# Selective scan of a Mamba layer on one Trainium2 core: one scan and one product per group of three units

## What is computed

```python
dA = jnp.exp(delta[..., None] * A)
dBu = delta[..., None] * Bm[:, :, None, :] * xc[..., None]

def step(h, inp):
    dA_t, dBu_t, C_t = inp
    h = dA_t * h + dBu_t
    y = jnp.einsum('bdn,bn->bd', h, C_t)
    return (h, y)
```

## Time and profile before

| | us |
|---|---|
| three runs | 6336.2, 6339.48, 6344.21 |
| median | 6339.48 |
| profiled execution: span from first to last instruction | 6343.7 |
| busy in this span: PE, DVE, POOL, ACT | 6036.5, 5685.5, 5209.8, 5097.3 |

### The profile page before, as it was taken

The page is one execution under the profiler, slowest core; times in us unless marked ns, Lnnn a source line. Parts: engine busy times, 40 slices in busy tenths (PEclk is TensorE's granted clock), DMA queues, the critical chain, the costliest instruction groups (busy, mean ns, idle before and its releaser), DMA issues. The chain is left out here.

```text
span 6343.7 us, 99100 instructions
## 1 busy us (share of the span) xinstructions
PE 6036.5 (95%) x32260; PEld 3123.0 (49%) x32260; DVE 5685.5 (90%) x4459; ACT 5097.3 (80%) x8658; POOL 5209.8 (82%) x5092
## 2 busy tenths in 40 slices
PE   8999999999999999999999999999999999998776
PEld 5645445454554545545455544545455454554222
DVE  0089999999999999999999999999999999999998
ACT  4588888888888888888888788888888888887664
POOL 0078888888888888888888888888888888888988
PEclk9999999999999999999999999999999999998665
DMA  3367676676767667675676767667676766767553
GB/s 95 88 165 170 160 167 157 163 162 169 169 154 168 155 165 170 155 182 142 167 162 162 173 156 169 155 164 163 167 169 156 166 154 165 168 142 160 129 124 75
DMA packets 805826, 983.25 MB, mean 155 GB/s; under 512 B 391258, under 2 KB 417542, under 8 KB 805318
## 3 DMA queue, kind: packets, MB, share of 16 engines
q1 hardware_dynamic: 805318, 976.92, 65.4%
HBM read 717.71 MB, written 259.00 MB: 154 GB/s over the span
## 5 line engine op out<-in xcount | busy, mean ns | idle before, releaser
L1181 POOL TENSOR_TENSOR hc<-hs,cs 128x512 f32<-128x512 f32 x3072 | 3835.6, 1271 | 692.7 <-DVE hs L1140 505.6
L1140 DVE TENSOR_TENSOR_SCAN hs<-av,state,b 128x512 f32<-128x512 f32 x2688 | 3257.8, 1263 | 88.6 <-POOL state L1185 4.9
L1008 ACT ACTIVATE av<-rep_d,nega 128x512 f32<-128x512 f32 x3072 | 2096.7, 713 | 41.5 <-DVE hs L1140 36.8
L1134 DVE TENSOR_TENSOR b<-rep_u,pb 128x1536 f32<-128x1536 f32 x1024 | 1803.5, 1761 | 211.0 <-PE pb L846 124.7
L855 PE MATMUL py<-hc,rsel 128*32 128x512 f32 x6144 | 1141.6, 634 | 40.6 <-POOL hc L1181 39.7
L769 PE MATMUL cb<-xu,w1a 96*128 96x392 f32 x2400 | 984.3, 513 | 27.7 <-DVE b1a L1120 17.4
L774 PEld LDWEIGHTS cb<-w2c,g 128*98 128x98 f32 x9600 | 885.9, 167 | 169.7 <-issue 106.9
L774 PE MATMUL cb<-w2c,g 128*98 128x96 f32 x9600 | 910.7, 252 | 17.4 <-ACT g L956 9.3
L956 ACT ACTIVATE g<-cb,b1a 128x392 f32<-128x392 f32 x1200 | 679.5, 579 | 87.0 <-PE cb L769 78.8
L810 PE MATMUL cb<-xn,wtap 96*96 96x512 f32 x1536 | 723.3, 607 | 2.4 <-ACT xn L1029 2.4
L769 PEld LDWEIGHTS cb<-xu,w1a 96*128 96x128 f32 x2400 | 414.5, 191 | 415.4 <-issue 199.3
(11 more groups left out here) (109 smaller groups left out, 6703.4 us busy)
## 6 DMA issues: line engine op xcount, KB each, us to landing
rep_d<-delta_scratch SPq DMA_DIRECT2D x512, 384.0 KB, 7.0
rep_u<-deltax_scratch SPq DMA_DIRECT2D x512, 384.0 KB, 6.3
cs<-c_scratch SPq DMA_DIRECT2D x512, 256.0 KB, 5.9
delta_scratch<-dlt SPq DMA_DIRECT2D x128, 384.0 KB, 3.1
deltax_scratch<-dlt SPq DMA_DIRECT2D x128, 384.0 KB, 9.2
t1r<-t_scratch SPq DMA_DIRECT2D x160, 240.0 KB, 6.5
v_scratch<-v2s SPq DMA_DIRECT2D x192, 192.0 KB
xb<-in_x SPq DMA_DIRECT2D x128, 192.0 KB, 4.6
```

The source lines that it names most:

```text
L1008: act.activation(av[:, n % NAV, :], rep_d[:, k % 2, j, :], ACT.Exp, scale=nega[:, q, j:j + 1])\
L1134: dve.tensor_tensor(b3[:, :, :], rep_u[:, k % 2, 3 * hf:3 * hf + 3, :], pb[:, None, :].broadcast_to([128, 3, T]), ALU.mult).then_inc(dve_b ...
L1140: dve.tensor_tensor_scan(hs[:, n % NHS, :], av[:, n % NAV, :], b3[:, n % 3, :], start, ALU.mult, ALU.add)\
L1181: pool.tensor_tensor(hc[:, n % NHC, :], hs[:, n % NHS, :], cs[:, k % 2, g % NQ, :], ALU.mult)\
```

## The change

Three scans of 512 columns become one scan of 3 x 512 = 1536 columns over the group. To keep the units apart, column 0 of every `av` tile is set to zero once and the exponentials write columns 1 to 511; so at the first column of each unit the running value is dropped. What the unit should have carried over is put into column 0 of b instead: b[0] plus a[0] times the state. For that POOL makes `first_x` = A times the first column of the next chunk's `rep_d`, ACT its exponential `first_a`, and POOL twice a chunk `carry` = `first_a` times `state`. In chunks 1 to 7 DVE then writes column 0 of b by a new instruction (`scalar_tensor_tensor`, `rep_u` times `pb` plus `carry`, 3 columns) and the other 511 columns by the product as before. In chunk 0 the product writes all columns.

POOL multiplies the group by C in one product of 1536 columns, after the one scan. `av` grows to 9 tiles, so that a group lies in one piece; two constant tables are stored more tightly to make room. The counts of the semaphores go from units to groups.

```diff
-NHC, NAV, NHS = 6, 8, 6
+NHC, NAV, NHS = 6, 9, 6
...
-    "act": dict(xn=10, y=(18, 6), d=11, mid=23, batch=16),
+    "act": dict(xn=10, y=(18, 6), d=11, mid=23, batch=16, first=15),
     "dve": dict(),
-    "pool": dict(u=23, bc=(18, 22), y=(17, 8)),
+    "pool": dict(u=23, bc=(18, 22), y=(17, 8), first=5, carry=(14, 23)),
...
-        up_w = sb("up_w", [128, 2, GW])
+        up_w = sb("up_w", [128, GW])
...
-        wdt = sb("wdt", [128, DI])
+        wdt = sb("wdt", [128, C])
...
-        state = sb("state", [128, NG, 3])
-        zero_state = sb("zero_state", [128, 1])
+        state = sb("state", [128, NQ, NJ])
+        first_x = sb("first_x", [128, NQ, NJ])
+        first_a = sb("first_a", [128, NQ, NJ])
+        carry = sb("carry", [128, NQ, NJ])
...
             def reduce(s, k, g):
-                pe.wait_ge(pool_hc, count(pool_hc, G * NU + 3 * g + 3))
+                pe.wait_ge(pool_hc, count(pool_hc, G * NG + g + 1))
...
-                act.wait_ge(dve_h, count(dve_h, G * NU + n + 1 - NAV))
-                act.activation(av[:, n % NAV, :], rep_d[:, k % 2, j, :], ACT.Exp, scale=nega[:, q, j:j + 1])\
+                act.wait_ge(dve_h, count(dve_h, G * NG + n // 3 + 1 - NAV // 3))
+                i = (G * NU + n) % NAV
+                act.activation(av[:, i, 1:T], rep_d[:, k % 2, j, 1:T], ACT.Exp, scale=nega[:, q, j:j + 1])\
                     .then_inc(act_a, 1)
...
+                if n == AT["act"]["first"] and 0 <= st.s and k + 1 < NC8:
+
+                    c = st.s * (NC8 - 1) + k
+                    act.wait_ge(pool_first, count(pool_first, c + 1))
+                    act.wait_ge(pool_carry, count(pool_carry, c * 2))
+                    act.activation(first_a[:, :, :], first_x[:, :, :], ACT.Exp).then_inc(act_first, 1)
...
-            dve.memset(zero_state[:, :], 0.0)
+            dve.memset(av[:, :, 0], 0.0).then_inc(av_set, 1)
...
             def unit(s, k, n):
                 G = s * NC8 + k
                 hf, g, q = n // 12, n // 3, n // 3 % NQ
+                if n % 3 != 0:
+                    return
+                js = slice(3 * hf, 3 * hf + 3)
...
-                if n % 3 == 0:
-
-                    dve.wait_ge(pe_b, count(pe_b, G * NG + g + 1))
-                    dve.wait_ge(dve_h, count(dve_h, G * NU + n))
-                    dve.tensor_tensor(b3[:, :, :], rep_u[:, k % 2, 3 * hf:3 * hf + 3, :],
-                                      pb[:, None, :].broadcast_to([128, 3, T]), ALU.mult).then_inc(dve_bu, 1)
-                    dve.wait_ge(pool_st, count(pool_st, G * NG + g + 1 - NHS // 3))
-                    dve.wait_ge(dve_bu, count(dve_bu, G * NG + g + 1))
-                dve.wait_ge(act_a, count(act_a, G * NU + n + 1))
-                start = state[:, g, n % 3:n % 3 + 1] if k > 0 else zero_state[:, 0:1]
-                dve.tensor_tensor_scan(hs[:, n % NHS, :], av[:, n % NAV, :], b3[:, n % 3, :], start, ALU.mult, ALU.add)\
+                dve.wait_ge(pe_b, count(pe_b, G * NG + g + 1))
+                dve.wait_ge(dve_h, count(dve_h, G * NG + g))
+                lo = 0
+                if k > 0:
+                    lo = 1
+                    dve.wait_ge(pool_carry, count(pool_carry, (s * (NC8 - 1) + k - 1) * 2 + hf + 1))
+                    dve.scalar_tensor_tensor(b3[:, :, 0], rep_u[:, k % 2, js, 0], pb[:, 0:1], carry[:, q, js],
+                                             ALU.mult, ALU.add).then_inc(dve_c, 1)
+                dve.tensor_tensor(b3[:, :, lo:T], rep_u[:, k % 2, js, lo:T],
+                                  pb[:, None, lo:T].broadcast_to([128, 3, T - lo]), ALU.mult).then_inc(dve_bu, 1)
+                dve.wait_ge(pool_st, count(pool_st, G * NG + g + 1 - NHS // 3))
+                dve.wait_ge(act_a, count(act_a, G * NU + n + 3))
...
+                a, h = (G * NU + n) % NAV, n % NHS
+                dve.tensor_tensor_scan(hs[:, h:h + 3, :].rearrange("p j t -> p (j t)"),
+                                       av[:, a:a + 3, :].rearrange("p j t -> p (j t)"),
+                                       b3[:, :, :].rearrange("p j t -> p (j t)"), 0.0, ALU.mult, ALU.add)\
                     .then_inc(dve_h, 1)
...
-                if n % 3 == 0:
-                    pool.wait_ge(pe_red, count(pe_red, G * NG + g + 1 - NHC // 3))
-                pool.wait_ge(dve_h, count(dve_h, G * NU + n + 1))
-                pool.tensor_tensor(hc[:, n % NHC, :], hs[:, n % NHS, :], cs[:, k % 2, g % NQ, :], ALU.mult)\
-                    .then_inc(pool_hc, 1)
-                if n % 3 == 2:
-
-                    pool.tensor_copy(state[:, g, :], hs[:, n % NHS - 2:n % NHS + 1, T - 1]).then_inc(pool_st, 1)
+                if n % 3 != 2:
+                    return
+                h, p = n % NHS - 2, n % NHC - 2
+                pool.wait_ge(pe_red, count(pe_red, G * NG + g + 1 - NHC // 3))
+                pool.wait_ge(dve_h, count(dve_h, G * NG + g + 1))
+                pool.tensor_tensor(hc[:, p:p + 3, :], hs[:, h:h + 3, :],
+                                   cs[:, k % 2, q, None, :].broadcast_to([128, 3, T]), ALU.mult).then_inc(pool_hc, 1)
...
+                if n == AT["pool"]["first"] and 0 <= st.s and k + 1 < NC8:
+
+                    p = (k + 1) % 2
+                    pool.wait_ge(rd_ld[p], count(rd_ld[p], st.s * (4 * 64) + ((k + 1) // 2 + 1) * 64))
+                    pool.wait_ge(act_first, count(act_first, ahead_of))
+                    pool.tensor_tensor(first_x[:, :, :], nega[:, :, :], rep_d[:, p, None, :, 0].broadcast_to([128, NQ, NJ]),
+                                       ALU.mult).then_inc(pool_first, 1)
+                if n in AT["pool"]["carry"] and 0 <= st.s and k + 1 < NC8:
+                    hf = AT["pool"]["carry"].index(n)
+                    js = slice(3 * hf, 3 * hf + 3)
+                    pool.wait_ge(act_first, count(act_first, ahead_of + 1))
+                    pool.wait_ge(pool_st, count(pool_st, G * NG + (hf + 1) * NQ))
+                    pool.tensor_tensor(carry[:, :, js], first_a[:, :, js], state[:, :, js], ALU.mult).then_inc(pool_carry, 1)
```

More of the change, by code:

```diff
@@ L346, in build @@
         act_a = sem("act_a")
+        av_set = sem("av_set")
+        pool_first = sem("pool_first")
+        act_first = sem("act_first")
+        pool_carry = sem("pool_carry")
+        dve_c = sem("dve_c")
         dve_bu = sem("dve_bu")
@@ L392, in build @@
             (bdt[:, 1:2], A["b_dt"][C:DI].rearrange("(c o) -> c o", o=1)),
-            (wdt[32:32 + RANK, :], A["WdtT"]), (wdt[96:96 + RANK, :], A["WdtT"]),
+            (wdt[32:32 + RANK, :], A["WdtT"][:, 0:C]), (wdt[96:96 + RANK, :], A["WdtT"][:, C:DI]),
             (wx[:, :, 0:RANK + 2 * DSTATE], A["WxT"].rearrange("(t p) e -> p t e", p=C)),
@@ L500, in _ @@
             load_xb(0, 0)
-            sp.dma_start(up_w[:, :, :], A["up_w"]).then_inc(ld_s, 16)
+            for r in range(2):
+                sp.dma_start(up_w[64 * r:64 * r + 64, :], A["up_w"][64 * r:64 * r + 64, r]).then_inc(ld_s, 16)
             load_xb(0, 1)
@@ L653, in c_part @@
                         sp.sem_inc(sp_passed, 1)
-                        sp.wait_ge(pool_hc, count(pool_hc, G * NU))
+                        sp.wait_ge(pool_hc, count(pool_hc, G * NG))
                         sp.sem_inc(sp_passed, 1)
@@ L689, in _ @@
         def _(pe):
-            pe.wait_ge(ld_s, count(ld_s, 32))
+            pe.wait_ge(ld_s, count(ld_s, 48))
             def setup():
@@ L741, in step @@
                     half = slice(64 * r, 64 * r + 64)
-                    mm = pe.matmul(bank[0:GW, 0:4 * C], up_w[half, r, :],
+                    mm = pe.matmul(bank[0:GW, 0:4 * C], up_w[half, :],
                                    xb[half, b % 2].rearrange("p i c -> p (i c)"), start=True, stop=True)
@@ L824, in batched @@
                 rows = slice(32 + 64 * t, 32 + 64 * t + RANK)
-                return pe.matmul(bank[0:C, :], wdt[rows, C * t:C * t + C], dbc[rows, :], start=True, stop=True)
+                return pe.matmul(bank[0:C, :], wdt[rows, :], dbc[rows, :], start=True, stop=True)
             def out(st, k, bank):
@@ L1138, in unit @@
-                dve.wait_ge(act_a, count(act_a, G * NU + n + 1))
-                start = state[:, g, n % 3:n % 3 + 1] if k > 0 else zero_state[:, 0:1]
-                dve.tensor_tensor_scan(hs[:, n % NHS, :], av[:, n % NAV, :], b3[:, n % 3, :], start, ALU.mult, ALU.add)\
+                    if G == 0:
+                        dve.wait_ge(av_set, count(av_set, 1))
+                dve.wait_ge(pe_b, count(pe_b, G * NG + g + 1))
+                dve.wait_ge(dve_h, count(dve_h, G * NG + g))
+                lo = 0
@@ new lines, in unit @@
+                dve.wait_ge(pool_st, count(pool_st, G * NG + g + 1 - NHS // 3))
+                dve.wait_ge(act_a, count(act_a, G * NU + n + 3))
+                if k > 0:
+                    dve.wait_ge(dve_c, count(dve_c, (s * (NC8 - 1) + k - 1) * NG + g + 1))
+                dve.wait_ge(dve_bu, count(dve_bu, G * NG + g + 1))
```

(24 more changed lines are left out.)

1 line of the change is left out of this document (added).

## The result

The changed kernel takes 8448.72 us (median of 4 runs, 8441.14 to 8454.08), against 6337.84 for the kernel before beside it. The ratio is 1.3327, with a 95% interval from 1.3308 to 1.3346. It is slower by a third, outside the predicted range of 6230 to 7300. The mechanism is that of rival B, but not at its price.

What follows compares the result with a forecast made beforehand. DVE and PE together were taken to bound the first fourteen samples, DVE alone the last two. Terms -92 + 98 + 10 + 35 = +51 on the profiled 6343.7 gave 6395, put at 6390 us by the runs' median; range 6230 to 7300.

Steps and rivals of the forecast that it cites:

- rival B: DVE's 3-column instruction, with two SBUF tensors, queues behind POOL's products: 7040 us, much slower; chance 0.33.
- the forecast: The prediction's own case for the whole kernel: four terms sum to +51 us, 6390 us, own range 6300 to 6490; chance 0.40.
- POOL's next product passes as well: Worse form of rival B: POOL's following product also goes ahead of DVE's 3-column instruction; 8,000 us and more.
- DVE's own work, -92: DVE: long scan 3.46 us against 3.62 for three, 3-column instruction adding 0.08 in 896 groups; ends +72 and -512.
- The third exponential, +98: Scan in a chunk's last group waits 2.0 us for ACT's third exponential, 98 times; half counted, ends 0 and 196.
- POOL and PE's sum, +10: POOL's single product starts after the whole scan, so hc reaches PE's sum later: +10 us, ends 0 and 770.
- first_x, +35: New wait in POOL's queue for rep_d's last quarter stalls DVE: 2.5 us a sample in fourteen samples, ends 0 and +120.
- rival A: PE and ACT come forward, so the exponential, POOL and PE waits vanish and -92 is left: 6248 us; chance 0.22.
- C: Rival: DVE's long scan saves nothing, taking 3.62 us like the three before: 6555 us; chance 0.05.

Runs made afterwards that it cites:

- e1: Changed kernel with the 3-column instruction reading a pb column (PSUM) in place of carry, state not carried between chunks: 6495.19 us, ratio 1.0239.
- e7: Kernel before, with only each of a group's three scans waiting for the group's third exponential instead of its own: 6367.19 us, ratio 1.0040.
- e11: e1 with first_x one group later in POOL's program (unit 8 instead of 5): 6381.86 us, ratio 1.0064 to the kernel before.
- e12: Kernel before, with only POOL's three one-unit products made one of 1536 columns behind the third scan: 6347.67 us, ratio 1.0004.
- e8: e4 with first_x one group later in POOL's program (unit 8 instead of 5): 6444.26 us, ratio 1.0163 to the kernel before.
- e4: Changed kernel with b's product over all columns and carry added in place by a second instruction with one SBUF tensor: 6557.26 us, ratio 1.0337.
- e3: Changed kernel with one more wait, for a copy long done, ahead of POOL's product: 8447.64 us, ratio 1.3316 to the kernel before.
- e13: Changed kernel with POOL writing one column of hc and waiting for that between scan and product: 6866.60 us, ratio 1.0828 to the kernel before.

## Why the prediction was wrong

**The step that failed** is the 3-column instruction. The forecast's sum holds it at 0.08 us a group, 72 us in all, with no wait behind POOL; it took 2.72 us on the mean, 2439 in all, and e1 shows that 1953 of the 2111 us lost hang on its second SBUF tensor. The reason for leaving the wait out stands in rival B: "After a scan DVE's next instruction starts 0.11 us later and POOL's product 0.15 later [...], so where both are ready DVE is first and nothing is lost." The starts were read rightly; what does not follow from them is "nothing is lost". In 422 groups DVE's record starts 50 to 59 ns ahead and DVE blocks all the same, 3.52 us each. B had priced only the cases in which POOL is ahead. That price, 2.9 us for each of 224 groups behind a statistic, was near: 189 pairs stand behind a statistic or its aggregate while the product runs, at 2.9. The 104 straight behind a scan in which DVE came 0.2 us or more late, at 3.3, it had not. The 8,000 that the prediction set aside for "POOL's next product passes as well" is near the result, by another way: what passes is the product of the same scan, and the one after it only in three groups (those behind the `dlt` product, 4.0 to 4.8 us each).

From that step came the second error, the choice of the forecast over B (0.40 against 0.33). The Trainium skill (SBUF — State Buffer, "Who interferes with whom") states the rule, and the prediction gave it: an instruction of DVE with two SBUF inputs and one of GpSimd that reads SBUF exclude each other for a whole instruction. The trace agrees, three columns against 1536 and all: the end of a blocked one lies 23 to 33 ns after the end of POOL's product. The same section says that the issue order decides who blocks; by the starts recorded in this trace that does not hold below 60 ns, where the one that starts second wins, 422 times of 422.

The terms of the forecast's sum, against the runs without the contention:

- **DVE's own work, -92.** Too small by 38 in DVE's own step, by two errors that cancel in part. The scan takes 3.353 us and not 3.46; the half throughput that the Trainium skill (DVE: opcode table, instruction layouts, handler registers and perf-mode slots, section on feedback) states for the scan's program, taken as two cycles a column, gave an estimate of 3.36, and the trace agrees. The 3 columns cost more: in e1 the most frequent step between b products is 5.467 us with them and 5.353 without, so 0.11 and not 0.08. Together (5.467 - 5.580) x 896 + (5.353 - 5.580) x 128 = -130 us.
- **The third exponential, +98.** The place was right, ahead of the last group of a chunk; alone it costs 25 us (e7), while DVE's waiting for PE's `pb` shrinks by 111 us against 156 of new waiting for `av`, which is what the lower end of that term was for. That it takes more beside the faster scan (243 us of DVE's waiting in e11, 156 in e7) the trace shows; how much of e11's time it is was not separated.
- **POOL and PE's sum, +10.** Right within the noise: +5 by the medians, with an interval from -3 to +9 (e12).
- **first_x, +35.** Too small by a factor of three: 113 us (e8 against e4, e11 against e1), near the far end of 120. The prediction took the fourteen samples at 2.5 us each. In e1 POOL waited in 89 of 112 chunks, 302.9 us, 3.4 each and up to 6.4 (in the change itself, slowed by the contention, 87.5 us in 46), where the prediction had read one chunk and counted two of a sample for its far end.
- **The sum.** Without the contention and nearly without first_x's wait the change is slower by 40 us (e11), where the sum had -92 + 98 + 10 = +16. With that wait back, and still without the contention, it is 6495 us (e1) against the forecast's 6390. With the sizes just measured the sum for e11 is -130 + 25 + 5 = -100, so some 140 us of DVE's saving does not reach the end, and rival A (6248) would not have come about either. In the first fourteen samples, 36 us longer than before in e11, PE is as full as before (busy 4897 us from 500 to 5500, before 4904); that this holds the saving back is read from the rows, and no run separates it. In the last two, which the prediction called DVE's alone, nothing is saved either (737.6 us in e11, 737.7 before): DVE waits there some 19 us for `av` and `pb`, against 3 before. C fell with the scan's 3.353 us.

## What to carry to other kernels

Count the SBUF tensors of every DVE instruction that runs beside POOL, however short it is: with the operand in PSUM the instruction took at most 0.23 us in all 896 groups (e1), and a scalar in SBUF beside one SBUF tensor did not wait either (the 3072 scans before, with `state` or `zero_state`, 1.25 to 1.28 us each). A second tensor can cost all of POOL's instruction that runs beside it, here 2.7 us on the mean for three columns. When two engines are released by the same event, a start order read a few hundredths of a microsecond apart is no order to build a price on; price the other order too. A wait for a DMA in an engine's queue is priced from all the chunks of the trace, not from the one that was looked at.

## What was not expected of the hardware

Which of the two goes first is not decided by which starts first in the records: POOL's product wins when it starts 50 to 59 ns after the DVE instruction (422 of 422 pairs; in e3 at 16 to 46 ns, 489 of 489), DVE when POOL starts 70 to 89 ns after it (159 of 159). No pair of this kernel lies between, and what sets the point is open. A POOL instruction that only writes, a memset of 0.10 us, does not block the DVE instruction beside it (e13), and put ahead of the product, with a wait for its end, it delays the product by enough to turn the order. The Trainium skill (SBUF — State Buffer, "Who interferes with whom") says the same of GpSimd instructions that only write, and the trace agrees.
